# Layout of an intermediate array: G kept rows first and fields last in a CIN tower

## The chip, the cores and the metric

The kernel runs on one core of one Trainium2 chip. A core has five engines that run side by side: TensorE (PE in the profile, with its weight loads as PEld), VectorE (DVE), ScalarE (ACT), GpSimd (POOL) and SyncE (SP), which here issues DMAs. TensorE's clock is granted at one of two levels, 1.2 or 2.4 GHz; the profile gives it as a share of full speed. The metric is the device time of one execution, in microseconds.

## The reference, cut to what matters

2048 rows of ids select 39 embedding vectors of 16 floats each. Two compressed interaction layers and a small MLP follow:

```
e  = stack of 39 table rows                       # [2048, 39, 16]
x1 = einsum('bid,hi->bhd', e x e, W0)             # [2048, 128, 16]
x2 = einsum('bid,hi->bhd', x1 x e, W1)            # i runs over 128 * 39
z  = concat(x1.sum(-1), x2.sum(-1))               # [2048, 256]
h  = relu(concat(z, dense_ctx) @ W_top1 + b1)     # 512
h  = relu(h @ W_top2 + b2)                        # 256
y  = h @ W_top3
```

Since only the sum of x2 over the 16 dimensions is wanted, layer 1 can be had from `G[i, b, f] = sum_d x1[b, i, d] * e[b, f, d]`, as 39 matmuls of 128 x 128 weights, one for each field f. A fortieth "field" of ones (f = 39) gives the sum of x1 itself.

## The kernel before, in words

The 2048 rows are taken in 8 iterations of 256 rows (`NB`), each of 8 chunks (c = 0 to 7) of 32 rows, so 64 chunks in all. A chunk has 512 columns (32 rows x 16 dimensions) and 7 steps (k = 0 to 6).

For each step TensorE or a DMA places shifted copies of the embeddings, VectorE multiplies them (`multiply`, L739), ScalarE rounds the product (`round_product`, L572), VectorE forms the remainder (`lower_part`, L748), and TensorE contracts both against W0 in three matmuls of 512 columns (`contract`, L397, L398, L400). The result x1 is copied out (`copy_x1`, L577), transposed (`transpose_x1`, L412), and split (L581, L759) in the chunk after. In that chunk's steps 3 to 6, `make_g` (L429) multiplies it with a block diagonal of the embeddings, in four parts q of 8 rows each: three matmuls give 320 columns, 8 rows of 40 fields, in PSUM. `copy_g` (L589) on ScalarE copies each part into G. G is in SBUF with 128 partitions (i) and holds two iterations' rows, 512, of 40 fields; the halves are used in turn. There are 64 x 4 = 256 such copies.

One iteration later `layer1` (L440) reads G: one fp32 matmul for each of the 39 fields, with the 256 rows of an iteration as moving operand. The table `LAYER1` places them in the chunks: 7 fields in c = 1, 4 in c = 2, 8 in each of c = 3, 4 and 5, and 4 in c = 6. `mlp1` (L459) reads field 39 of G as moving operand for each of the four blocks of 128 of the first MLP layer, in c = 6 and 7; `mlp2` (L471) and `mlp3` (L480) run in c = 0 of the iteration after. Iteration 0 has no layer 1. The last iteration's layer 1 and MLP stand after all chunks, with nothing beside them.

A fp32 matmul of this program is two instructions on TensorE: 39 fields in 8 iterations are 312 calls, and the profile has 624 instructions of L440. The four G matmuls of `mlp1` are 64 instructions in the same way.

At c = 2 to 3 and c = 6 to 7 the embeddings of the next tile of 128 rows are split on VectorE (`split_hi`, L716, and `split_lo`, L722), transposed on TensorE (L368) and copied by ScalarE in four copies (`copy_eT`, L556). This happens for 15 tiles beside the chunks.

Each engine has its own instruction list, written out by hand in the order of these steps, and engines wait for each other's semaphores. The start of the kernel uses the memory of G as `staging` for weights, before any G is written.

Of the kernel before, what the change touches and what calls it, by code (L numbers as in the profile page):

```python
# [5 lines left out]
F = 39  # L22
D = 16
B = 2048
H = 128
# [6 lines left out]
CB = 32  # L32
# [4 lines left out]
NB = TB * TPI  # L37
ITERS = B // NB
Q = COLS // 128
QB = CB // Q  # L40
FO = F + 1
# [26 lines left out]
def after(engine, semaphore, value):  # L68

    if isinstance(value, int) and value <= 0:  # L70
        return
    engine.wait_ge(semaphore, value)
# [45 lines left out]
def cin_tower(nc, dense_t, ids, tables, w_top1, b_top1, w_top2, b_top2, w_top3, w0, w1,  # L118
# [5 lines left out]
    with ctx:  # L124
        def sb(name, shape, dt=f32):
            return ctx.enter_context(nc.sbuf_tensor(name, shape, dt))

        def ps(name, shape, dt=f32):
            return ctx.enter_context(nc.psum_tensor(name, shape, dt))

        def sem(name):
            return ctx.enter_context(nc.semaphore(name))
# [7 lines left out]
        w1T = sb("w1T", [H, F, H])  # L140
        wt1_cin = sb("wt1_cin", [128, 2, H1])

        wt1_dense = sb("wt1_dense", [3 * GAP, H1], f32r)
# [18 lines left out]
        x1T_lo = sb("x1T_lo", [128, Q, H], f32r)  # L162
        e_diag = [sb(f"e_diag{n}", [128, QB, Q, 2, FO], f32r) for n in range(2)]

        G = sb("G", [H, FO, 2 * NB])

        staging = G[:, :, :].rearrange("p f b -> p (f b)")
        w0_both = staging[0:ROWS, 0:2 * KT * H].rearrange("p (a k h) -> p a k h", a=2, k=KT)
        w0_sum = w0_both[:, 0, :, :]
        wt1_dense_f = staging[0:3 * GAP, 2 * KT * H + SELECTED:2 * KT * H + SELECTED + H1]  # L170
# [1 line left out]
        dense_parts = sb("dense_parts", [3 * GAP, NB], f32r)  # L172
# [13 lines left out]
        g_ps = [ps(f"g_ps{n}", [128, QB * FO]) for n in range(2)]  # L186
        mlp_ps = ps("mlp_ps", [128, 2, NB])
# [38 lines left out]
        g_ready = sem("g_ready")  # L226
# [129 lines left out]
        def _(pe):  # L356
# [76 lines left out]
            def layer1(it, fields):  # L433

                for j in fields:
                    if j == 0:

                        pe.wait_ge(g_ready, Q * CPI * (it + 1))
                        after(pe, y_ready, it)
                    last = nc.tensor.matmul(mlp_ps[:, 0, :], w1T[:, j, :], G[:, j, bass.ds(it % 2 * NB, NB)],  # L440
                                            start=(j == 0), stop=(j == F - 1))
                    if j == F - 1:
                        last.then_inc(z2_in_ps, 1)

            def mlp1(it, third):

                if third == 0:

                    pe.wait_ge(z2_ready, it + 1)
                    pe.wait_ge(dense_split, it + 1)  # L450
                if third == 3:

                    pe.wait_ge(h1_ready, it * M1 + 2)
                operands = ((wt1_cin[:, 0, :], G[:, F, bass.ds(it % 2 * NB, NB)]), (wt1_dense[:, :], dense_parts[:, :]),
                            (wt1_cin[:, 1, :], z2[:, :]))
                for n in (2 * third, 2 * third + 1):
                    m, part = n // 3, n % 3
                    weights, x = operands[part]
                    last = nc.tensor.matmul(mlp_ps[:, m % 2, :], weights[:, m * 128:(m + 1) * 128], x,  # L459
                                            start=(part == 0), stop=(part == 2))  # L460
                if third % 3 == 2:
                    last.then_inc(h1_in_ps, 1)
# [20 lines left out]
            def chunk(it, c, first=False, second=False, final=False):  # L483
# [6 lines left out]
                for k in range(KT):  # L490

                    for item in ITEMS_AT[k]:
                        if item < REPS:
                            replicate(it, c, item)
                        elif has_next:
                            replicate(*chunk_after(it, c), item - REPS)
                    if makes_eT and (c % CPT, k) in ET_STEPS:
                        if (c % CPT, k) == ET_STEPS[0]:

                            after(pe, x1T_lo_ready, it * CPI + c)  # L500
                        transpose_e(next_tile, ET_STEPS.index((c % CPT, k)))
                    if has_last:
                        if k == 1:
                            transpose_x1(*last, final and c >= CPT)
                        if k >= KT - Q:
                            make_g(*last, k - (KT - Q), final and c >= CPT)
                    if not first:
                        layer1(it - 1, fields_at(c, k))
                        if (c, k) in MLP1_STEPS:
                            mlp1(it - 1, MLP1_STEPS.index((c, k)))  # L510
                    if not first and not second:
                        if (c, k) in MLP2_STEPS:
                            mlp2(it - 2, MLP2_STEPS.index((c, k)))
                        if (c, k) == MLP3_STEP:
                            mlp3(it - 2)
                    contract(it, c, k)
# [26 lines left out]
            for q in range(Q):  # L543
                make_g(end, CPI - 1, q)
            layer1(end, range(F))
            for n in range(len(MLP1_STEPS)):
                mlp1(end, n)
# [5 lines left out]
        def _(act):  # L553
# [29 lines left out]
            def copy_g(it, c, q):  # L583

                if q == Q - 1:
                    act.wait_ge(e_diag_free, it * CPI + c + 3)
                else:
                    act.wait_ge(g_in_ps, (it * CPI + c) * (Q - 1) + q + 1)
                nc.scalar.copy(G[:, :, bass.ds(it % 2 * NB + c * CB + q * QB, QB)].rearrange("i f b -> i b f"),  # L589
                               g_ps[q % 2][:, :].rearrange("i (b f) -> i b f", f=FO)).then_inc(g_ready, 1)  # L590

            def copy_z2(it):

# [23 lines left out]
            def chunk(it, c, first=False, second=False, final=False):  # L617
# [5 lines left out]
                for k in range(KT):  # L623
                    if k + 1 < KT:
                        round_product(it, c, k + 1)
                    elif has_next:
                        round_product(*chunk_after(it, c), 0)
                    if k == 0 and has_last:
                        copy_x1(*last)
                    if REPS in ITEMS_AT[k] and has_next:  # L630
                        copy_cycle(*chunk_after(it, c))

                    c1, k1 = (c, k - 1) if k else (c - 1, KT - 1)
                    if makes_eT and (c % CPT, k) in ET_STEPS:
                        copy_eT((c // CPT + 1) % TPI, next_tile, ET_STEPS.index((c % CPT, k)))
                    if k > KT - Q and has_last:
                        copy_g(*last, k1 - (KT - Q))
                    if k == 0 and not (first and c <= 1):
                        copy_g(*chunk_before(*last), Q - 1)
                    if not first and c1 >= 0:  # L640
                        if len(fields_at(c1, k1)) and fields_at(c1, k1)[-1] == F - 1:
                            copy_z2(it - 1)
                        if (c1, k1) in MLP1_STEPS[2::3]:
                            relu1(it - 1, MLP1_STEPS[2::3].index((c1, k1)))
                    if not first and not second and (c1, k1) == MLP2_STEPS[-1]:
                        relu2(it - 2)
                    if k == 1 and has_last:
                        round_x1T(*last)
                    if (c, k) == DENSE_STEP and not first:
                        round_dense(it - 1)  # L650
                    if (c, k) == MLP3_STEP and not first and not second:
                        copy_y(it - 2)
# [14 lines left out]
            for c in range(CPI):  # L667
                chunk(end, c, final=True)
            copy_x1(end, CPI - 1)
            copy_g(end, CPI - 2, Q - 1)  # L670
            relu2(end - 1)
            round_x1T(end, CPI - 1)
# [169 lines left out]
```

## Time and profile before

| | us |
|---|---|
| median of 3 runs | 965.97 |
| lowest, highest | 965.49, 969.34 |
| profiled execution: span of core 0 | 1508.4 |
| PE busy in it | 884.9 |
| DVE busy | 648.8 |
| ACT busy | 600.9 |
| mean granted TensorE clock | 0.788 |

For the profiled execution no time but its span is given. It is 542 us above the median of the timed runs: it has long stretches in which all engines stand still and for which the trace shows no releaser ("another core or an unknown queue" in the chain, "remote" or "issue" as releaser). The stretches between them run without a stop, and these are the ones to read. Durations of instructions overlap where an engine is pipelined, so the time that one really takes on its engine is read from start to start, or from the chain of waits, which counts each moment once.

### The profile page before, as it was taken

To read this page: it belongs to the slowest core of one execution; us is meant where nothing else is said; L and a number is where in the kernel's file an instruction comes from. 1 tells how busy PE (TensorE), PEld (TensorE's weight loads), DVE (VectorE), ACT (ScalarE), POOL (GpSimd) and SP (SyncE) were. 2 spreads that over 40 slices of the span, in tenths; PEclk is the share of its full clock that TensorE was granted. 3 is DMA by queue.
4 is the path that set the end of the run, shared out by engine and by line. 5 is a ranking of instruction groups with operands and counts; after the bars stand their busy time and mean duration, and the time that the engine had idled before them with its cause. 6 is when DMAs were issued, how large, how long until landed. Compare 5 with 4: busy or idle time off the path is not lost.

```text
span 1508.4 us, 15925 instructions
## 1 busy us (share of the span) xinstructions
PE 884.9 (59%) x3824; PEld 686.1 (45%) x3824; DVE 648.8 (43%) x1012; ACT 600.9 (40%) x1033; POOL 623.7 (41%) x628
## 2 busy tenths in 40 slices
PE   0136393719268292763958367291863936629998
PEld 0014262508146181552846256270642724527886
DVE  2015292617155282442835156160632615427870
ACT  0013282407154171532735154160532714418772
POOL 6756437461714517154271715417054071450000
PEclk9997596759678596785977678595775967859999
DMA  4112142212122132122322122121221312203320
GB/s 130 24 39 61 38 113 52 69 45 66 26 75 61 23 98 68 38 52 51 85 59 58 27 77 71 39 67 25 78 59 18 95 27 70 67 13 101 106 78 3
DMA packets 101439, 88.81 MB, mean 59 GB/s; under 512 B 59925, under 2 KB 71325, under 8 KB 101250
## 3 DMA queue, kind: packets, MB, share of 16 engines
q1 hardware_dynamic: 81410, 83.02, 18.8%
q0 software_dynamic: 19968, 5.15, 3.9%
q14 instruction: 45, 0.37, 0.1%
q8 instruction: 16, 0.26, 0.1%
HBM read 21.35 MB, written 10.49 MB: 21 GB/s over the span
## 4 chain that ended last, share of the span: by engine, by line
PE 38%; another core or an unknown queue 28%; issue 20%; ACT 6%; DVE 4%; POOL 2%; DMA 1%; DVEq 0%; ACTq 0%; SPq 0%; POOLq 0%
PE mlp_ps L440 7%; PE g_ps L429 6%; PE x_ps L400 5%; PE x_ps L397 5%; PE x_ps L398 5%; PE rep_ps L386 3%; POOL e_rows L346 2%; ACT G L589 2%; PE mlp_ps L471 2%; PE mlp_ps L459 2%; DVE products L739 2%; ACT product_hi L572 2%; DVE product_lo L748 1%; PE aux_ps L368 1%
## 5 line engine op out<-in xcount | busy, mean ns | idle before, releaser
L346 POOL DMA_INDIRECT e_rows<-in_tbl_dram,ids_sb x624 | 623.5, 999 | 721.3 <-DMA ids_sb<-in_ids_dram 535.7
L748 DVE TENSOR_TENSOR product_lo<-products,product_hi 117x512 fp32r<-117x512 f32 (+1 forms) x448 | 308.1, 688 | 598.7 <-remote 369.6
L572 ACT CAST product_hi<-products 117x512 fp32r<-117x512 f32 (+1 forms) x448 | 281.4, 628 | 298.7 <-remote 131.2
L400 PE MATMUL x_ps<-product_lo,w_hi 117*128 117x512 f32 (+1 forms) x448 | 199.3, 445 | 176.0 <-issue 91.8
L397 PE MATMUL x_ps<-product_hi,w_hi 117*128 117x512 f32 (+1 forms) x448 | 254.7, 569 | 9.9 <-issue 9.9
L589 ACT COPY G<-g_ps 128x320 f32 (+1 forms) x256 | 189.4, 741 | 38.2 <-remote 24.6
L400 PEld LDWEIGHTS x_ps<-product_lo,w_hi 117*128 117x128 f32 (+1 forms) x448 | 92.5, 207 | 224.1 <-issue 104.5
L398 PE MATMUL x_ps<-product_hi,w_lo 117*128 117x512 f32 (+1 forms) x448 | 190.3, 425 | 0.0
L429 PE MATMUL g_ps<-e_diag,x1T_hi 128*128 128x320 f32 x512 | 134.7, 347 | 92.6 <-issue 58.9
L440 PE MATMUL mlp_ps<-G,w1T 128*128 (+1 forms) x624 | 186.8, 400 | 0.8 <-ACT G L589 0.8
L429 PEld LDWEIGHTS g_ps<-e_diag,x1T_hi 128*128 128x128 f32 x512 | 97.6, 206 | 126.9 <-issue 82.7
L368 PE MATMUL aux_ps<-ident,e_parts 128*80 128x128 f32 x256 | 47.3, 316 | 178.1 <-ACT eT L556 84.5
L556 ACT CAST eT<-aux_ps 80x512 fp32r<-80x512 f32 x64 | 67.5, 1054 | 198.8 <-issue 95.0
L739 DVE TENSOR_TENSOR products<-rep_ps,left 117x512 f32<-117x512 f32 x192 | 131.1, 683 | 33.2 <-issue 20.4
L386 PE MATMUL rep_ps<-eT,select_r 80*117 80x512 f32 (+1 forms) x256 | 117.9, 461 | 41.4 <-issue 22.9
L739 DVE TENSOR_TENSOR products<-shifted,left 117x512 f32<-117x512 f32 (+1 forms) x192 | 131.7, 686 | 0.2
L368 PEld LDWEIGHTS aux_ps<-ident,e_parts 128*80 128x80 f32 x256 | 31.6, 137 | 198.2 <-issue 151.6
L440 PEld LDWEIGHTS mlp_ps<-G,w1T 128*128 128x128 f32 x624 | 115.7, 201 | 11.4 <-ACT G L589 1.0
L412 PE MATMUL aux_ps<-ident,x 128*128 128x128 f32 x256 | 45.7, 308 | 113.0 <-issue 104.0
L397 PEld LDWEIGHTS x_ps<-product_hi,w_hi 117*128 117x128 f32 (+1 forms) x448 | 93.8, 209 | 25.1 <-issue 13.5
L398 PEld LDWEIGHTS x_ps<-product_hi,w_lo 117*128 117x128 f32 (+1 forms) x448 | 94.5, 211 | 11.5
L759 DVE TENSOR_TENSOR x1T_lo<-aux_ps,x1T_hi 128x512 fp32r<-128x512 f32 x64 | 44.3, 692 | 118.5 <-issue 60.5
(42 smaller groups left out, 612.7 us busy)
## 6 DMA issues: line engine op xcount, KB each, us to landing
shifted<-cycle SPq DMA_DIRECT2D x128, 234.0 KB
left<-cycle SPq DMA_DIRECT2D x192, 78.0 KB
e_scratch<-e_parts SPq DMA_DIRECT2D x16, 640.0 KB
e_diag<-e_scratch SPq DMA_DIRECT2D x512, 20.0 KB
e_rows<-in_tbl_dram,ids_sb POOLq DMA_INDIRECT x624
shifted<-cycle SPq DMA_DIRECT2D x64, 156.0 KB
w1T<-in_L_rec_W_dram SPq DMA_DIRECT2D x1, 2496.0 KB
G<-in_L_rec_W_dram SPq DMA_DIRECT2D x1, 819.0 KB
```

The source lines that it names most:

```text
L346: nc.gpsimd.indirect_dma_start(out=e_rows[slot][:, f * D:(f + 1) * D], out_offset=None, in_=tables[f], in_offset=bass.IndirectOffsetOnAxis ...
L368: last = nc.tensor.transpose(aux_ps[0:2 * FO, m * TB:(m + 1) * TB], e_parts[:, n * DPB + m, :, :].rearrange("b q f -> b (q f)"), ident[:, :])
L386: nc.tensor.matmul(rep_ps[rep_bank(c, item)][0:rows, :], select_r[:, item:item + rows], columns(c), start=True, stop=True).then_inc(rep_in ...
L397: nc.tensor.matmul(x1_ps[c % 2][:, :], w0_hi[0:rows, k, :], product_hi[0:rows, slot, :], start=(k == 0), stop=False)
L398: nc.tensor.matmul(x1_ps[c % 2][:, :], w0_lo[0:rows, k, :], product_hi[0:rows, slot, :], start=False, stop=False)
L400: last = nc.tensor.matmul(x1_ps[c % 2][:, :], w0_hi[0:rows, k, :], product_lo[0:rows, (c * KT + k) % LO_RING, :], start=False, stop=(k == ...
L429: last = nc.tensor.matmul(g_ps[q % 2][:, :], x[:, q, :], e_diag[c % 2][:, :, q, part, :], start=(n == 0), stop=(n == 2))
L440: last = nc.tensor.matmul(mlp_ps[:, 0, :], w1T[:, j, :], G[:, j, bass.ds(it % 2 * NB, NB)], start=(j == 0), stop=(j == F - 1))
L572: nc.scalar.copy(product_hi[0:rows, n % RING, :], products[0:rows, n % RING, :]).then_inc(hi_ready, 1)
L589: nc.scalar.copy(G[:, :, bass.ds(it % 2 * NB + c * CB + q * QB, QB)].rearrange("i f b -> i b f"), g_ps[q % 2][:, :].rearrange("i (b f) -> ...
L739: nc.vector.tensor_tensor(products[0:rows, n % RING, :], x[0:rows, :], left[c % 2][0:rows, :], ALU.mult).then_inc(product_ready, 1)
L748: nc.vector.tensor_tensor(product_lo[0:rows, n % LO_RING, :], products[0:rows, n % RING, :], product_hi[0:rows, n % RING, :].bitcast(f32), ...
```

## The change

G is declared with the rows ahead of the fields. ScalarE's copy then writes 320 consecutive floats where it wrote each float 2048 bytes from the one before it (within a row's 40 fields). TensorE's moving operand for a field, which was 256 consecutive floats, is now 256 floats with 160 bytes from one to the next. The size of G, the staging area, the order of all instructions and all semaphores are as they were.

```diff
-        G = sb("G", [H, FO, 2 * NB])
-
-        staging = G[:, :, :].rearrange("p f b -> p (f b)")
+        G = sb("G", [H, 2 * NB, FO])
+
+        staging = G[:, :, :].rearrange("p b f -> p (b f)")
...
-                    last = nc.tensor.matmul(mlp_ps[:, 0, :], w1T[:, j, :], G[:, j, bass.ds(it % 2 * NB, NB)],
+                    last = nc.tensor.matmul(mlp_ps[:, 0, :], w1T[:, j, :], G[:, bass.ds(it % 2 * NB, NB), j],
                                             start=(j == 0), stop=(j == F - 1))
...
-                operands = ((wt1_cin[:, 0, :], G[:, F, bass.ds(it % 2 * NB, NB)]), (wt1_dense[:, :], dense_parts[:, :]),
+                operands = ((wt1_cin[:, 0, :], G[:, bass.ds(it % 2 * NB, NB), F]), (wt1_dense[:, :], dense_parts[:, :]),
                             (wt1_cin[:, 1, :], z2[:, :]))
...
-                nc.scalar.copy(G[:, :, bass.ds(it % 2 * NB + c * CB + q * QB, QB)].rearrange("i f b -> i b f"),
-                               g_ps[q % 2][:, :].rearrange("i (b f) -> i b f", f=FO)).then_inc(g_ready, 1)
+                nc.scalar.copy(G[:, bass.ds(it % 2 * NB + c * CB + q * QB, QB), :].rearrange("i b f -> i (b f)"),
+                               g_ps[q % 2][:, :]).then_inc(g_ready, 1)
```

## Rows read from the trace of the kernel before

**Rows 1.** The page: span, busy time of each engine, shares of the chain.

```profile
span 1508.4 us, 15925 instructions
...
PE 884.9 (59%) x3824; PEld 686.1 (45%) x3824; DVE 648.8 (43%) x1012; ACT 600.9 (40%) x1033; POOL 623.7 (41%) x628
...
PE 38%; another core or an unknown queue 28%; issue 20%; ACT 6%; DVE 4%; POOL 2%; DMA 1%; DVEq 0%; ACTq 0%; SPq 0%; POOLq 0%
```

**Rows 2.** Stretches: start:end, length, engines' busy time and instructions, PE clock, DMA.

```profile
194.53:203.99 9.46, 9.28 (x43) 6.41 (x42) 9.19 (x17) 7.94 (x16) 0.00 (x0) 1.00 0.40 112
1186.23:1200.55 14.32, 14.31 (x61) 11.16 (x61) 10.10 (x17) 9.21 (x18) 0.00 (x0) 0.88 0.27 74
1388.27:1399.28 11.01, 11.01 (x56) 9.51 (x55) 9.46 (x15) 8.09 (x14) 0.00 (x0) 1.00 0.27 73
1399.28:1412.13 12.85, 12.66 (x68) 9.77 (x67) 11.18 (x17) 10.28 (x17) 0.00 (x0) 1.00 0.39 112
1412.13:1423.69 11.56, 11.39 (x57) 9.59 (x56) 9.46 (x15) 8.94 (x16) 0.00 (x0) 1.00 0.40 117
1435.15:1446.60 11.45, 11.45 (x58) 9.89 (x57) 9.47 (x15) 8.19 (x14) 0.00 (x0) 1.00 0.29 79
1457.74:1467.73 9.99, 9.99 (x52) 8.46 (x51) 6.97 (x11) 7.68 (x16) 0.00 (x0) 1.00 0.20 53
1476.85:1493.97 17.12, 17.10 (x78) 14.73 (x78) 0.41 (x1) 0.41 (x1) 0.00 (x0) 1.00 0.01 2
```

**Rows 3.** Chain of waits, 1435 to 1447: start, us on the chain, what.

```profile
1435.34 0.87 PE mlp_ps L440 x4
1436.21 0.23 PE x_ps L397
...
1437.13 0.44 PE aux_ps L412 x4
...
1440.06 0.43 PE g_ps L429 x3
```

**Rows 4.** Chain of waits, 1406 to 1414.

```profile
1407.16 0.77 ACT G L589
1407.94 0.24 ACT product_hi L572
...
1408.26 1.07 ACT eT L556
1409.33 0.56 ACT G L589
1409.88 0.26 ACT product_hi L572
...
1411.27 0.57 ACT G L589
```

**Rows 5.** Groups by line and shape: count, busy us, mean ns, idle before.

```profile
L589 ACT COPY G<-g_ps 128x320 f32 x160 | 118.6, 741 | 31.2 <-remote 22.4 <-issue 5.6 <-PE g_ps L429 2.8
...
L577 ACT COPY x<-x_ps 128x512 f32<-128x512 f32 x64 | 37.4, 585 | 136.1 <-remote 82.8 <-issue 29.7 <-PE x_ps L400 23.5
...
L722 DVE TENSOR_TENSOR e_parts<-e_rows,e_parts 128x624 f32<-128x624 f32 x16 | 19.6, 1222 | 0.0
...
L716 DVE CAST e_parts<-e_rows 128x624 fp32r<-128x624 f32 x16 | 11.4, 716 | 39.9 <-DMA e_rows<-in_tbl_dram,ids_sb 39.9
...
L596 ACT COPY h<-mlp_ps 128x256 f32<-128x256 f32 x8 | 3.3, 411 | 15.8 <-PE mlp_ps L440 15.8
...
L698 DVE TENSOR_TENSOR G<-G 117x896 f32<-117x896 f32 x1 | 1.1, 1093 | 0.0
...
L706 DVE TENSOR_TENSOR wt_dense<-G,wt_dense 32x512 fp32r<-32x512 f32 x1 | 0.7, 684 | 0.0
...
L700 DVE CAST w_hi<-G 117x896 fp32r<-117x896 f32 x1 | 0.6, 627 | 0.0
...
L704 DVE CAST wt_dense<-G 96x512 fp32r<-96x512 f32 x1 | 0.4, 416 | 0.0
```

## The prediction, made before the changed kernel was run

> **What bounds the kernel now.** I read the page first. The span is 1508.4 us against a median of 966, and the chain names an unknown releaser or "issue" for 48% of it [rows 1]. Busy shares of the span therefore say little: 884.9 us of PE is 59% of this span but 92% of 966. So I looked for stretches without a stop and cut them at the starts of the copy of x1, which comes once per chunk; one stretch is then one chunk [rows 2].
>
> The last iteration shows seven such chunks at full granted clock (1.00). The chunk at 1388.27 is c = 1 (11.01 us), 1399.28 is c = 2 (12.85), 1412.13 is c = 3 (11.56), 1435.15 is c = 5 (11.45) and 1457.74 is c = 7 (9.99). PE is busy for the whole of c = 1 and c = 5, while ACT has 8.1 to 8.2 us and DVE 9.5 us. Busy PE can still be a PE that waits, so the chain of waits decides: in c = 5 it stays on PE from matmul to matmul. A 512-column matmul of the contraction holds it for 0.23 us, three 320-column ones 0.43 to 0.45, and four layer-1 instructions 0.87, so 0.217 each [rows 3]. The sum of a chunk with 8 fields: 21 contractions and 4 replications at 0.23 are 5.75 us, 12 for G 1.8, 4 transposes 0.44 [rows 3], 16 for layer 1 3.47. That is 11.46, and the stretch is 11.45. TensorE bounds these chunks, and what is added to a matmul there is added to the time.
>
> Chunk c = 2 is another case. Its sum for PE, with 8 instructions of layer 1 and 12 transposes of e, is about 11.0, yet it takes 12.85, and from 1407 to 1412 the chain runs on ACT: copy of G, rounding of a product, copy of eT, again and again, with 0.56 us of each round on the copy of G [rows 4]. An eT group is made for 15 tiles. Iteration 0 has no layer 1, and there DVE is busy 9.19 of 9.46 us [rows 2]: neither side of the change reaches it but through that same ACT queue.
>
> These stretches account for most of the timed 966 us. Seven iterations of 92 to 99 us (the last one's chunks, and in the loop more at its turn, as in the 14.32 us of a c = 0) and iteration 0 at 9.46 us a chunk [rows 2], with some 118 us ahead of the first copy of x1 and 41 behind the last come to about 916; I take the other 50 as lying around the span or as small stops. The differences below apply to the profiled span and the median alike (1508.4 and 966), as the unexplained stops hold none of the instructions that change.
>
> **Part 1, ScalarE's copy.** 256 copies of 128 x 320 now take 741 ns each. Copies from PSUM that write in one piece take 411 ns for 256 columns and 585 for 512 [rows 5]: 0.68 ns a column, which gives an estimate of 455 for 320. So a copy shortens by 286 ns, and ACT loses 73 us of busy time. In chunks on PE's chain this is worth nothing: the copies lie beside matmuls, and the next part of G waits for the copy two parts before, 1.5 us earlier. On the ACT chain of an eT group three copies stand: at most 3 x 0.286 = 0.86 us, at least 0, since DVE (11.18 busy) and PE (11.0) are next. Both lie 1.7 us below the 12.85, so I take most of it, 0.7. Over 15 groups that is 10.5 us gained, with ends 0 and 12.9.
>
> **Part 2, TensorE's reads.** 688 instructions (624 of layer 1, 64 of mlp1) read 256 fp32 values, consecutive before and 160 bytes apart after. A column of these takes 0.217 us / 256 = 0.85 ns; a contraction's takes 0.23 / 512 = 0.45 [rows 3]. No row shows TensorE reading apart, so I bound it by the other engines. VectorE's subtraction L722 reads one operand 64 bytes apart: 624 elements in 1222 ns. The consecutive ones take 1093 ns for 896 and 684 for 512, so 1.065 ns an element and 139 fixed; for L722 that leaves 1.74 ns an element. The cast L716 reads the same way with one operand: consecutive casts, 627 ns for 896 and 416 for 512, have 0.55 ns an element and 135 fixed, so 581 / 624 = 0.93 ns. The scattered copy of G writes an element every (741 - 237) / 320 = 1.58 ns, with the fixed part of the other copies [rows 5]. So:
> - Low end: TensorE gets a value in less than its 0.85 ns a column already, and the reads cost nothing.
> - Cast's rate: 0.93 ns, +0.02 us an instruction.
> - Subtraction's rate: 1.74 ns, and an instruction takes 0.445 instead of 0.217: +0.23. The scattered copy's 1.58 ns gives +0.19.
> - High end: its 0.85 ns a column may hide two fetches of each value (a contraction's column needs half the time). At 1.74 ns each that is 0.89 us an instruction, +0.67.
>
> The nearest is the pair in the middle, two rows of fp32 data in which each element is far from the next. The same price comes from two fetches at 0.85 to 0.93 ns. I take 1.70 ns and +0.216 us, double the present time.
>
> The Trainium skill, Advanced Engine Details and Errata, section Memory Cachelines, says that SBUF is read in lines of 16 bytes, that two hits on a line are needed to hide the access, and that a new line at every access costs a penalty; it gives no size. Here every value would be in a line of its own, where four shared one. The rows on VectorE and ScalarE agree in direction, and they disagree among themselves on size (0.93 against 1.74). By that rule the copies gain and the matmuls lose; without it only the copies' gain would be left. FP8 and Floating Point Precision, section TensorE Precision Notes, says that true fp32 is four passes through the array. With two instructions a call, as the counts here show, that would be two passes in each. Whether a pass fetches its values again, neither page nor trace tells.
>
> **Sum.** Per iteration with layer 1: c = 1 has 14 instructions, c = 3, 4 and 5 have 48; all 62 on PE's chain: 13.4 us. c = 2 and 6 have 16 and mlp1 8 more in c = 6 and 7: 24 x 0.216 = 5.2, of which I let half vanish in the slack of the ACT stretches: 2.6. Together 16.0, for 7 iterations 112. Behind the last chunk, 78 instructions stand bare, 17.12 us now [rows 2], and 8 of mlp1: 86 x 0.216 = 18.6. Less the 10.5 of part 1: +120. So 966 + 120 = 1086 for the median, and 1508 + 120 = 1628 for a profiled span with the same stops. What is late next in the chunks is nothing new: PE holds the chain for longer, ACT and DVE wait more. No wait is added and no queue changes.
>
> **Rivals.**
> - A, the reads are free, and the kernel is faster: a value comes within 0.85 ns. For it: the cast's 0.93 ns is nearly there, and fp32 columns have double the time of the contraction's. Against it: L722. Then only part 1 is left: 966 - 10.5 = 955.5, in a range of 950 to 963.
> - B is my forecast, 1086; by itself 1055 to 1115 (1.58 to 1.74 ns; none or all of the 5.2 us hidden).
> - C, two slow fetches: 688 x 0.65 = 447, less 10 and a little hidden: about 1395. It needs the high end twice, which no row asks for.
> - D, a small price between free and double. At the cast's rate, 0.02 x 688 = 13 us, less 10.5: 968. At half of B's price, 0.108: about 1020.
> - E, the copy doesn't shorten because what slows it is the read of PSUM and not the write. The read is consecutive in both kernels, so I give it no more than a few in 100, inside the others; it takes the 10.5 away.
>
> Slower than before is decided by one thing: above some 0.02 us more an instruction (0.93 ns a column) the matmuls eat the copies' gain.
>
> **How the numbers follow.** B 0.42, A 0.37, D 0.13, C 0.08. Within 0.5%, 4.8 us, is about what a measurement of this kernel can't tell from no change. A is faster by more than that in 0.30 and not in 0.07; D is half way to the same in 0.04; the rest is slower: 0.30, 0.11, 0.59. The likeliest is B: 1086 us. The range has to reach A: 953 to 1110, which leaves out C, A's lowest edge and B's highest. B alone would be 1055 to 1115.
>
> **What would show it.** In the profile after: L589 near 455 ns (not 741), which decides E. Four instructions of L440 on the chain 1.74 us instead of 0.87, the 78 bare ones in 34 us instead of 17.12, and a chunk with 8 fields 14.9 us instead of 11.45: B. Unchanged 0.87 and 17.12 would be A, 2.6 or more C. Iteration 0 stays at 9.5 us. In an eT chunk, ACT off the chain and less than 12.85 us would confirm part 1 in A; in B the chain there moves to PE. The prediction is wrong if L440's spacing stays below 0.3 us.

## The result and the profile after

The changed kernel took 1104.03 us (median of 4 runs, 1100.08 to 1105.47) against 965.73 for the kernel before (4 runs, 963.87 to 969.34): a ratio of 1.1428, with an interval of 1.1394 to 1.1462. That is 138 us slower. Forecast were 1086 us, and 953 to 1110 as the range.

Lines of the code stand 16 lower in the profile after: L424 is what was L440, L573 was L589, L330 was L346. The page of the changed kernel first (busy time and share by engine, the clock in 40 slices, the head of the chain by engine):

```profile
span 1103.7 us, 15925 instructions
...
PE 981.1 (89%) x3824; PEld 657.0 (60%) x3824; DVE 656.1 (59%) x1012; ACT 539.8 (49%) x1033; POOL 647.1 (59%) x628
...
PEclk9997979999989999999999999999999999999999
...
PE 76%; POOL 15%; issue 7%; ACT 1%; DVE 0%; DMA 0%; DVEq 0%; ACTq 0%; POOLq 0%
```

This execution has no long stops, unlike the first one of the kernel before [rows 1], so its span can be set beside the timed runs. PE has 76% of the chain.

The two edits show in the groups by line of the changed kernel (count, busy us, mean ns):

```profile
L573 ACT COPY G<-g_ps 128x320 f32 x160 | 69.9, 437 | 2.9
...
L443 PE MATMUL mlp_ps<-G,wt_cin 128*128 x40 | 23.6, 681 | 0.2
```

The copy takes 437 ns, where [rows 5] had 741 and the estimate was 455. For the matmuls the mean is not the occupancy, so the chain of waits is the view, here in a chunk c = 5 of the changed kernel (start, us on the chain):

```profile
998.01 2.00 PE mlp_ps L424 x4
1000.00 0.23 PE x_ps L381
...
1000.94 0.44 PE aux_ps L396 x4
1001.38 0.99 PE mlp_ps L424 x2
```

Four instructions of layer 1 hold TensorE for 2.00 us; in [rows 3] four held it for 0.87. Everything else between them is unchanged: 0.23 a contraction, 0.44 for four transposes. The stretches of the changed kernel that answer to [rows 2] (length, busy time by engine, clock, DMA) are one whole iteration, c = 5 in it, the c = 2 of the last iteration, and the bare 78 instructions of the end:

```profile
680.26:803.52 123.26, 120.52 (x479) 81.86 (x479) 81.34 (x127) 67.35 (x130) 80.48 (x78) 0.99 0.33 85
755.71:771.71 16.00, 16.00 (x58) 10.25 (x57) 9.74 (x15) 7.22 (x15) 12.19 (x12) 1.00 0.28 71
951.45:965.90 14.45, 14.25 (x67) 9.86 (x66) 11.31 (x17) 9.69 (x17) 0.00 (x0) 1.00 0.34 105
1047.78:1087.04 39.26, 39.24 (x78) 16.44 (x78) 0.41 (x1) 0.41 (x1) 0.00 (x0) 1.00 0.01 2
```

The 78 instructions take 39.26 us instead of 17.12, so 0.503 each instead of 0.219: a price of 0.284 us. With 16 of them a chunk of 8 fields should grow by 4.54 us, and it grew from 11.45 to 16.00, by 4.55. The c = 2 of the last iteration grew from 12.85 to 14.45. The clock is at its upper level (1.00) in the two chunks and at the end, and PE is busy for 14.25 of the 14.45 us, so the chain has moved to it there.

But 688 instructions at 0.284 us are 195 us, and the kernel lost 138. The copies' gain is small; some 50 us are missing. That became the main question.

### The profile page after: what moved, and what is told of

Same layout as the page of the kernel before. It is cut to its first block, busy times and chain, and to the rows that moved or that the text cites. A ratio compares the mean times of both kernels' runs of the same rounds, so it can differ in the third digit from the quotient of the medians.

```text
span 1103.7 us, 15925 instructions
## 1 busy us (share of the span) xinstructions
PE 981.1 (89%) x3824; PEld 657.0 (60%) x3824; DVE 656.1 (59%) x1012; ACT 539.8 (49%) x1033; POOL 647.1 (59%) x628
## 4 chain that ended last, share of the span: by engine, by line
PE 76%; POOL 15%; issue 7%; ACT 1%; DVE 0%; DMA 0%; DVEq 0%; ACTq 0%; POOLq 0%
PE mlp_ps L424 27%; POOL e_rows L330 15%; PE g_ps L413 8%; PE x_ps L381 8%; PE x_ps L384 8%; PE x_ps L382 8%; PE rep_ps L370 5%; PE mlp_ps L443 4%; PE mlp_ps L455 3%; PE aux_ps L352 2%; PE aux_ps L396 2%; PE mlp_ps L464 1%; ACT h L590 0%; DVE products L723 0%; ACT G L573 0%
## 5 line engine op out<-in xcount | busy, mean ns | idle before, releaser
L330 POOL DMA_INDIRECT e_rows<-in_tbl_dram,ids_sb x624 | 646.9, 1037 | 283.7 <-issue 186.8
L556 ACT CAST product_hi<-products 117x512 fp32r<-117x512 f32 (+1 forms) x448 | 279.5, 624 | 314.8 <-PE x_ps L384 176.0
L424 PE MATMUL mlp_ps<-G,w1T 128*128 (+1 forms) x624 | 351.4, 674 | 0.5 <-ACT G L573 0.5
L381 PE MATMUL x_ps<-product_hi,w_hi 117*128 117x512 f32 (+1 forms) x448 | 311.7, 696 | 0.0
L384 PE MATMUL x_ps<-product_lo,w_hi 117*128 117x512 f32 (+1 forms) x448 | 180.5, 403 | 1.6 <-DVE product_lo L732 1.2
L382 PE MATMUL x_ps<-product_hi,w_lo 117*128 117x512 f32 (+1 forms) x448 | 179.3, 400 | 0.0
L370 PE MATMUL rep_ps<-eT,select_r 80*117 80x512 f32 (+1 forms) x256 | 108.7, 425 | 53.5 <-DVE products L723 49.9
L424 PEld LDWEIGHTS mlp_ps<-G,w1T 128*128 128x128 f32 x624 | 112.8, 195 | 45.4 <-issue 37.9
L413 PE MATMUL g_ps<-e_diag,x1T_hi 128*128 128x320 f32 x512 | 122.7, 321 | 0.3 <-issue 0.2
L573 ACT COPY G<-g_ps 128x320 f32 (+1 forms) x256 | 111.4, 435 | 4.2 <-PE g_ps L413 1.2
L370 PEld LDWEIGHTS rep_ps<-eT,select_r 80*117 80x117 f32 (+1 forms) x256 | 47.8, 187 | 78.8 <-DVE products L723 61.0
L413 PE MATMUL g_ps<-e_diag,x1T_lo 128*128 128x320 f32 x256 | 80.0, 312 | 0.0
```

Of the source, the lines that this page charges most:

```text
L330: nc.gpsimd.indirect_dma_start(out=e_rows[slot][:, f * D:(f + 1) * D], out_offset=None, in_=tables[f], in_offset=bass.IndirectOffsetOnAxis ...
L370: nc.tensor.matmul(rep_ps[rep_bank(c, item)][0:rows, :], select_r[:, item:item + rows], columns(c), start=True, stop=True).then_inc(rep_in ...
L381: nc.tensor.matmul(x1_ps[c % 2][:, :], w0_hi[0:rows, k, :], product_hi[0:rows, slot, :], start=(k == 0), stop=False)
L382: nc.tensor.matmul(x1_ps[c % 2][:, :], w0_lo[0:rows, k, :], product_hi[0:rows, slot, :], start=False, stop=False)
L384: last = nc.tensor.matmul(x1_ps[c % 2][:, :], w0_hi[0:rows, k, :], product_lo[0:rows, (c * KT + k) % LO_RING, :], start=False, stop=(k == ...
L413: last = nc.tensor.matmul(g_ps[q % 2][:, :], x[:, q, :], e_diag[c % 2][:, :, q, part, :], start=(n == 0), stop=(n == 2))
```

## The experiments

Two theories were set against each other. **P** is the account of the prediction: TensorE, and ScalarE in the eT groups, bound the kernel before. **G** was formed from the profile after: the gather on GpSimd bounds the kernel before in its timed runs, and part of what the matmuls now take was waiting for gathered rows before.

**The two halves of the change, alone.** For the copy alone, the reads were made consecutive again:

```diff
-                    last = nc.tensor.matmul(mlp_ps[:, 0, :], w1T[:, j, :], G[:, bass.ds(it % 2 * NB, NB), j],
+                    last = nc.tensor.matmul(mlp_ps[:, 0, :], w1T[:, j, :], G_flat[:, bass.ds(it % 2 * (NB * FO) + j * NB, NB)],
...
```

(The operand of `mlp1` is changed in the same way.)

> The copy of G writes in one piece as after the change; TensorE reads 256 consecutive values as before it, from the same half of G, so the values it takes belong to other fields and rows and the output is not the reference's. Theory P (the prediction's account: TensorE and, in the eT groups, ScalarE bound the kernel before): copies of 435 ns instead of 741, 10.5 us less, about 955.5 us. Theory G (in the timed runs the gather on GpSimd bounds the kernel before: 39 gathers of about 1.34 us a tile are 52 us, 104 us an iteration of two tiles, and an unstopped iteration of the rest takes only 92 to 99): the copies lie in that slack, and the time stays within 3 us of 966.

Measured: 964.63 us (958.26 to 968.69, 10 runs) against 969.71, ratio 0.9952 (0.9917 to 0.9987). For the reads alone, the copy scatters again:

```diff
-                nc.scalar.copy(G[:, bass.ds(it % 2 * NB + c * CB + q * QB, QB), :].rearrange("i b f -> i (b f)"),
-                               g_ps[q % 2][:, :]).then_inc(g_ready, 1)
+                rows = G_halves[:, bass.ds(it % 2, 1), :, c * CB + q * QB:c * CB + (q + 1) * QB]
+                nc.scalar.copy(rows.rearrange("i h f b -> i h b f"),
+                               g_ps[q % 2][:, :].rearrange("i (h b f) -> i h b f", h=1, f=FO)).then_inc(g_ready, 1)
```

> TensorE reads values 160 bytes apart as after the change; the copy of G scatters as before it (1024 bytes apart, within one iteration's half of G), so the output is not the reference's. Theory P: the reads alone cost what the whole change costs plus the 10.5 us that the copies give: about 1114 us. Theory G: TensorE bounds every chunk once its reads are slow, ScalarE's queue is hidden, and the time is within 5 us of the changed kernel's 1104. Both: L424's instructions 0.50 us apart on the chain.

Measured: 1109.41 us (1108.62 to 1113.91, 4 runs), ratio 1.1457 (1.1382 to 1.1533). The whole loss is in the reads. Both halves fall between the theories: a gain of 5 us from the copy (the interval is 1 to 8) where P said 10.5 and G up to 3, and 1109 where P said 1114 and G 1104 within 5. The intervals leave out P's 10.5 for the copy, but a gain smaller than forecast doesn't name what bounds the kernel, so these two runs don't settle the base.

**Another profile of the kernel before.** No edit.

> The kernel before, unchanged, for a profile without the long stops of the first. Theory P: span about 950, chunks with 8 fields of 11.45 us throughout, the iteration at 92 to 99 us, GpSimd idle between tiles. Theory G: the same chunks, but an iteration of 104 us, GpSimd without a pause from its first gather to its last near 840 us, and VectorE's split waiting for gathered rows once or twice an iteration.

Measured: 962.99 us, span 961.2. This execution has none of the stops. Its line of the gather, and whom VectorE waited for, from its groups by shape:

```profile
L346 POOL DMA_INDIRECT e_rows<-in_tbl_dram,ids_sb x624 | 658.2, 1055 | 192.8 <-issue 188.7 <-DMA ids_sb<-in_ids_dram 4.1
...
L716 DVE CAST e_parts<-e_rows 128x624 fp32r<-128x624 f32 x16 | 11.2, 699 | 109.3 <-DMA e_rows<-in_tbl_dram,ids_sb 109.1
```

GpSimd idles 188.7 us in gaps of 0.3 between gathers and only 4.1 us for ids: 658.2 + 192.8 = 851 us without a pause, 53 a tile and 106 an iteration. VectorE's split of e waits 109.1 us for gathered rows, of which 39.9 are the first tile, at the start of the kernel. Two chunks of this execution, a c = 5 and the c = 6 after it, which holds a split:

```profile
674.59:686.04 11.45, 11.45 (x58) 9.90 (x57) 9.54 (x15) 8.27 (x15) 9.01 (x9) 1.00 0.39 92
686.04:707.01 20.97, 15.79 (x69) 12.49 (x68) 11.26 (x17) 10.75 (x18) 16.09 (x17) 0.84 0.41 111
```

The first is the chunk of [rows 2]; the second takes 20.97 us, where the same kind of chunk takes 13.28 in the next experiment. PE is busy for 15.79 us of it, where such a chunk of the next experiment has PE busy for 13.29, and the granted clock of this stretch is 0.84: for a part of it the clock is at its lower level, and the matmuls take longer. That is in the price of the wait too. The chain of waits between 300 and 850 us says the same (shares by line):

```profile
by line: POOL e_rows L346 44.0%; issue 17.3%; PE g_ps L429 4.3%; PE mlp_ps L440 4.0%; PE x_ps L400 3.8%; PE x_ps L397 3.8%; PE x_ps L398 3.7%; PE rep_ps L386 2.9%; PE mlp_ps L471 2.1%; PE mlp_ps L459 2.0%; DMA ids_sb<-in_ids_dram 1.4%; DMA 
```

**Fewer gathers, in both kernels.** From the second iteration on, 20 of 39 gathers a tile, with the semaphore values to match:

```diff
-                    for f in range(F):
+                    for f in range(fields):
...
-                sp.wait_ge(gathered[slot], (it + 1) * (16 * F))
+                sp.wait_ge(gathered[slot], it * (16 * GATHERED) + 16 * F)
```

> The kernel before with 20 of 39 gathers per tile from the second iteration on (the other fields keep old rows, so the output is not the reference's); semaphore values to match. GpSimd's 104 us an iteration fall to about 54. Theory G: the time falls from 966 to the sum of unstopped stretches, 900 to 920 us. Theory P: the gathers are hidden anyway, and the time stays within 5 us of 966.

> The changed kernel with 20 of 39 gathers per tile from the second iteration on, in the same way (output not the reference's). Both theories: TensorE bounds it, so the time stays within 10 us of 1104. Under Theory G the difference to the run before it is then the whole price of the reads less the copies' gain, 688 x 0.283 = 195 us less about 10: 185 us, where the full kernels differ by only 138. Under Theory P it is the 138 of the full kernels.

Measured: the kernel before falls to 896.4 us (894.26 to 898.63, 4 runs; ratio 0.9283, 0.9240 to 0.9326) and the changed one to 1082.75 (1081.34 to 1085.2, 4 runs; ratio to the kernel before with all gathers 1.1215, 1.1165 to 1.1264). P allowed the first 5 us of change, and it was 69. G forecast 900 to 920 there, so the fall was 4 us larger than its range, and no change in the second; the second fell by 21, more than the 10 allowed. The reason is at the start: iteration 0 has no layer 1, so its chunks are short in both kernels, and the gather bounds the changed kernel there too. From copy of x1 to copy of x1, its iterations 0 and 1 took 112.1 and 131.5 us with all gathers and 99.6 and 122.0 with 20, the later ones 123 and 123. The difference of the two is 186 us against 138 with all gathers. An iteration of the kernel before with 20 gathers, and one of the changed kernel with 20, in their stretches, each with its c = 0 behind it:

```profile
564.86:663.59 98.73, 96.39 (x478) 78.63 (x478) 79.81 (x127) 74.39 (x131) 42.26 (x40) 1.00 0.38 103
564.86:577.55 12.69, 12.68 (x61) 9.95 (x61) 9.96 (x17) 9.21 (x18) 0.00 (x0) 1.00 0.29 78
```

```profile
658.32:781.03 122.71, 120.33 (x479) 81.83 (x479) 81.13 (x127) 67.34 (x130) 41.66 (x40) 0.99 0.30 83
658.32:672.35 14.03, 14.03 (x61) 11.08 (x61) 10.09 (x17) 8.28 (x18) 0.00 (x0) 0.88 0.26 74
```

98.7 us is less than the 106 of two full tiles' gathers; 122.7 is more. The c = 0 chunks read nothing from G, and yet one takes 1.34 us more: its granted clock was 0.88. So 1.3 of the 24 us between these two iterations are clock and not reads. A c = 0 of 14 us is no mark of the reads: with 20 gathers it comes in four of the five iterations 1 to 5 of the changed kernel and in two of those of the kernel before. And the chain of the kernel before with 20 gathers, 300 to 780 us, has no gather in it:

```profile
by line: PE mlp_ps L441 16.1%; PE g_ps L430 12.9%; PE x_ps L401 11.8%; PE x_ps L398 11.6%; PE x_ps L399 11.4%; PE rep_ps L387 7.6%; issue 6.9%; PE mlp_ps L460 3.8%; PE mlp_ps L472 3.6%; PE aux_ps L413 3.2%; ACT G L590 2.7%; PE aux_ps L369 2
```

So theory G stands and P falls as to the base. The unloaded difference, 186, is the reads' 195 less some 6 to 9 for the copies. Even the 896 us hold some of the gather's wait: tile 1 is still gathered whole, and VectorE waits 13.6 us for it in the c = 2 of iteration 0.

**The copy without the gather in front.** The copy in one piece and consecutive reads, with 20 gathers.

> Copy in one piece, consecutive reads (values of other fields and rows), and 20 of 39 gathers from the second iteration on: part 1 of the change without the gather's cover. To be set against the kernel before with 20 gathers, 896 us. The prediction's term of 10.5 us (0.7 us in each of 15 eT groups) holds if it is 884 to 888; if ScalarE's queue is worth less than the chain of waits suggested, 890 to 896.

Measured: 890.37 us (890.06 to 891.69, 4 runs). The ratio to the full kernel before, timed beside it, is 0.9197 (0.9166 to 0.9228) here and 0.9283 (0.9240 to 0.9326) for scattered copies. That is 6.0 us less in medians, just inside the range of the weaker account, and 8.3 by the ratios. The c = 2 chunks shrink by half a microsecond, not by 0.7, and those of c = 6 by 0.3; over 7 iterations that is 5.8. A c = 2 with scattered copies, and one with copies in one piece:

```profile
489.82:502.71 12.89, 12.85 (x68) 9.85 (x67) 11.23 (x17) 10.30 (x18) 9.85 (x10) 1.00 0.44 117
```

```profile
486.97:499.34 12.37, 12.30 (x67) 9.66 (x66) 11.35 (x17) 9.55 (x17) 9.49 (x10) 1.00 0.40 109
```

This run and the changed kernel with 20 gathers differ only in TensorE's reads: 890.37 against 1082.75, or 192 us in medians and 195 in the ratios. That is the full 688 times 0.284, with nothing hidden.

**What the distance costs.** Layer 1's fields read with eight different steps, and fp32r matmuls are added at the end.

```diff
+                    if j < 5:
+                        last = nc.tensor.matmul(mlp_ps[:, 0, :], x, apart(it, 1), **ends)
+                    elif j < 10:
+                        last = nc.tensor.matmul(mlp_ps[:, 0, :], x, apart(it, 2), **ends)
...
+            for n in range(12):
+                nc.tensor.matmul(x1_ps[n % 2][:, 0:NB], w0_hi[0:ROWS, n % KT, :], narrow(10), start=True, stop=True)
```

> Layout as after the change, but the 39 layer-1 matmuls read G with other steps between values: fields 0 to 4 with 4 bytes, then five fields each with 8, 16, 20, 32, 40, 80 and the last four with 160 bytes (wrong values, so the output is not the reference's). At the very end 72 extra matmuls of 256 fp32r columns read an fp32r tile with steps of 4, 8, 16, 20, 32 and 40 bytes. Theory Lines (a value in a new 16-byte line costs a fixed time): 0.22 us an instruction at 4 and 8 bytes, 0.50 from 16 bytes on, alike for 16 to 160. Theory Distance (cost grows with the step): 16 to 40 bytes stay below 0.35 us and 160 is the dearest. On the fetches: if an fp32 instruction fetches each value twice, the fp32r matmul (half the time per column when consecutive, about 0.11 to 0.12 us) takes 0.25 us with values apart; if it fetches each once, the fp32r one takes 0.50 us like the fp32 one.

The one run took 1069.59 us. The chain of waits over the bare part at the end has, in order, steps of 4, 8, 16, 20, 32, 40, 80 and 160 bytes for fp32 (L434 to L448), then 4, 8, 16, 20, 32 and 40 for fp32r (L559 to L569):

```profile
1004.23 2.43 PE mlp_ps L434 x10
1006.66 2.25 PE mlp_ps L436 x10
1008.91 4.53 PE mlp_ps L438 x10
1013.44 4.57 PE mlp_ps L440 x10
1018.00 4.61 PE mlp_ps L442 x10
1022.62 4.53 PE mlp_ps L444 x10
1027.15 5.33 PE mlp_ps L446 x10
1032.48 4.01 PE mlp_ps L448 x8
...
1051.84 1.60 PE x_ps L559 x12
1053.44 2.75 PE x_ps L561 x12
1056.19 2.80 PE x_ps L563 x12
...
1064.35 3.20 PE x_ps L569 x12
```

For fp32: 0.225 us an instruction at 8 bytes, close to the 0.219 of the consecutive reads in [rows 2] (the first ten here, 0.243 each, include the start of the stretch), then a jump to 0.453 at 16, flat to 40 (0.453 to 0.461), 0.533 at 80 and 0.501 at 160. Theory Lines holds for the place of the jump; its claim of one price for all steps does not, as 80 and 160 bytes cost 0.05 to 0.08 more. For fp32r the jump comes already at 8 bytes: 0.133 to 0.229.

**The same tile, both types.** To exclude that the two types differed by tile, fp32 and fp32r matmuls read one tile with steps of 4, 8, 12 and 16 bytes.

```diff
+                nc.tensor.matmul(x1_ps[n % 2][:, 0:NB], w1T[0:ROWS, n, :], narrow(2).bitcast(f32), start=True, stop=True)
...
+                nc.tensor.matmul(x1_ps[n % 2][:, 0:NB], w0_hi[0:ROWS, n % KT, :], narrow(2), start=True, stop=True)
```

> The kernel before, with matmuls of 256 columns added at the very end that all read the same tile (e_diag) with steps of 4, 8, 12 and 16 bytes: first as fp32 (12 instructions each), then as fp32r (12 each). Told apart: whether fp32 and fp32r differ by tile or by type. By type: fp32 0.22, 0.22, 0.22 to 0.45, 0.45 us; fp32r 0.12, 0.23, 0.23, 0.23. By tile: fp32 on this tile shows a cost at 8 bytes already. If an fp32 instruction fetched every value twice in two passes like the fp32r one, 8 bytes would cost it 2 x 0.23 = 0.46; if that stays 0.22, the account of two plain passes is out.

The one run took 996.27 us. The chain at its end, fp32 first (L556 to L562), then fp32r (L564 to L570):

```profile
969.38 2.79 PE x_ps L556 x12
972.16 2.70 PE x_ps L558 x12
974.87 4.08 PE x_ps L560 x12
978.95 5.44 PE x_ps L562 x12
984.38 1.40 PE x_ps L564 x12
985.79 2.74 PE x_ps L566 x12
988.53 2.81 PE x_ps L568 x12
991.34 2.80 PE x_ps L570 x12
```

It is by type. fp32: 0.233, 0.225, 0.340 and 0.453 us. At 8, 12 and 16 bytes 256 values lie in 128, 192 and 256 lines of 16 bytes, and the times are 1.76, 1.77 and 1.77 ns a line. Consecutive values lie in 64 lines and take nearly as long as at 8 bytes, so there something other than the lines sets the time. fp32r: 0.117, 0.228, 0.234 and 0.233, which is 0.9 ns a value for any step but 4 (the run before had 0.218 us at 32 bytes and 0.267 at 40), and no price by lines. The time of fp32 at 8 bytes stays at 0.225, so two plain passes that each pay what fp32r pays (0.46) are out. What makes the two types differ is left open.

**Pairs.** The rate at 8 bytes points to a layout between the two, fields in pairs:

```diff
-        G = sb("G", [H, 2 * NB, FO])
+        G = sb("G", [H, FO // 2, 2 * NB, 2])
...
-                    last = nc.tensor.matmul(mlp_ps[:, 0, :], w1T[:, j, :], G[:, bass.ds(it % 2 * NB, NB), j],
+                    last = nc.tensor.matmul(mlp_ps[:, 0, :], w1T[:, j, :], G[:, j // 2, bass.ds(it % 2 * NB, NB), j % 2],
...
-                nc.scalar.copy(G[:, bass.ds(it % 2 * NB + c * CB + q * QB, QB), :].rearrange("i b f -> i (b f)"),
-                               g_ps[q % 2][:, :]).then_inc(g_ready, 1)
+                nc.scalar.copy(G[:, :, bass.ds(it % 2 * NB + c * CB + q * QB, QB), :].rearrange("i g b s -> i b g s"),
+                               g_ps[q % 2][:, :].rearrange("i (b g s) -> i b g s", g=FO // 2, s=2)).then_inc(g_ready, 1)
```

> A layout between the two: G is [H, 20, 512, 2], fields in pairs, so that TensorE reads 256 values 8 bytes apart (0.22 us an instruction in the run on steps, as when consecutive) and ScalarE writes pairs, 160 separate places a copy where the kernel before has 320. The whole computation is done. If a place costs ScalarE what it does in the kernel before, half of 306 ns is saved: about 590 ns a copy. Theory G: the gather still bounds the kernel, the gain is part of the 5 us that the copy alone gave: 961 to 966 for 966, a ratio of 0.995 to 1.000. Theory P: about 5 us, 961. If 8 bytes cost TensorE in layer 1 after all, it is above 1000.

Measured: 970.42 us (966.09 to 978.8, 12 runs) against 968.88, ratio 1.0023 (0.9994 to 1.0052): no gain over the kernel before. Its groups by shape show the copy's new price and the wait for rows, and its chain shows the 78 bare instructions of layer 1:

```profile
L573 ACT COPY G<-g_ps 128x320 f32 x160 | 73.3, 458 | 0.9
...
L700 DVE CAST e_parts<-e_rows 128x624 fp32r<-128x624 f32 x16 | 11.2, 698 | 128.2 <-DMA e_rows<-in_tbl_dram,ids_sb 128.2
```

```profile
938.15 17.86 PE mlp_ps L424 x78
```

The copy takes 458 ns and not 590: writing two floats together takes almost all of the scatter's price away. TensorE pays a little: 17.86 us for the 78 instructions that took 17.12, so 0.229 each instead of 0.219, an estimate of 6.5 us for all 688. VectorE waits 128.2 us for gathered rows, 19 more than in the second profile of the kernel before. GpSimd's own unbroken time, busy and idle, and the span were 851.0 and 961.2 us in that profile, 856.0 and 965.7 with the copy alone, and 860.0 and 970.5 here: each time the span is 110 us more than the gather's, and the differences between the three are how fast the gathers went. The 5 us of the copy alone therefore can't be found in the profiles. So the same layout was run with 20 gathers, beside the kernel before with 20.

> The layout in pairs with 20 of 39 gathers from the second iteration on (the other fields keep old rows). If the pairs give what the copy in one piece gives where no gather stands in front: 889 to 892 us, as the run with copies in one piece (890) and 5 to 7 below the kernel before with 20 gathers (896). If the pairs gain nothing even there: 894 to 899.

> The kernel before with 20 of 39 gathers again, on the same chip as the run with pairs, so that the two can be compared: 894 to 899 us.

Measured: 894.73 us (893.63 to 895.79, 4 runs) and 897.94 (897.33 to 899.21, 4 runs). That is 3.2 us less, and the two sets of runs don't overlap; the ratios to the full kernel, 0.9221 (0.9173 to 0.9269) and 0.9255 (0.9207 to 0.9303), do. The time itself lies in the range that was expected if the pairs gain nothing (894 to 899), and the difference of 3.2 falls short of the 5 to 7 that were expected if they gain what the copy in one piece does. The slightly dearer reads would explain that: the copy in one piece with consecutive reads had 890.37. No version run here with all its gathers is surely faster than the kernel before by over 0.5%.

## Why the prediction came out as it did

**The likeliest case was the right one.** Case B, reads at about double the time of a matmul, was forecast at 1086 us, and 1104 came; the 2.00 us of four instructions are 2.3 times the 0.87 before. Cases A (free), C (two slow fetches, 1395) and D are out by the same 2.00 us. E is out by the copy's 437 ns.

**The price of an instruction was mis-sized**: 0.216 us forecast, 0.284 measured. VectorE's subtraction, at 1.74 ns a value [rows 5], was a good neighbour for steps of 16 to 40 bytes (0.453 / 256 = 1.77 ns). It says nothing of the further 0.05 us an instruction at 160 bytes; no row with such a distance between reads was there. The cast's 0.93 ns was the wrong neighbour for fp32; fp32r with steps of 12 and 16 bytes has that rate (0.91).

**The sum over an iteration was mis-sized as well.** Without the gather's cover an iteration grew from 98.7 to 122.7 us, by 24, where 16.0 was forecast. At the measured price, the 62 instructions on PE's chain are 17.6 us, and the 24 others 6.8; the copies give back 0.8 (c = 2 and c = 6), and the lower clock in c = 0 adds 1.3 in the pair compared, together 24.9 for the 24.0 measured. "I let half vanish" was too kind: of the 24 others' 6.8 us some 0.9 vanished at most, and the 192 to 195 us between the two runs that differ only in the reads leave as little. With faster copies PE is busy for 12.30 of the 12.37 us of a c = 2, so no slack is left there for slower reads. The bare end grew by 22.1 for its 78 instructions alone, where 18.6 was forecast for 86.

**The step that failed is the first one**, "These stretches account for most of the timed 966 us". The prediction summed them to 916 and took "the other 50 as lying around the span or as small stops". Around the span lie 1.8 us (962.99 timed, 961.2 of span), and there are no small stops. The 916 also hold 118 us ahead of the first copy of x1, where the undisturbed profile has 81.3, and 9.46 us for every chunk of iteration 0, where c = 2 takes 27.6 even with 20 gathers. With 20 gathers the kernel takes 896 us, and the other 70 were the gather, which ran without a pause. Its numbers stood in the groups by line of that first profile (count, busy us, mean ns, idle before and its releasers):

```profile
L346 POOL DMA_INDIRECT e_rows<-in_tbl_dram,ids_sb x624 | 623.5, 999 | 721.3 <-DMA ids_sb<-in_ids_dram 535.7 <-issue 185.6
```

623.5 us busy and 185.6 of issue gaps are 809 us for 16 tiles, 101 an iteration, more than the 92 to 99 of the chunks. The prediction cut out stretches between stops and summed them, and so cut out the engine whose work had been done during the stops. In that execution GpSimd waited 535.7 us for ids, which looked like slack; in the undisturbed one it waited 4.1.

**The two errors offset each other.** The forecast was 130.6 us for the reads (112 and 18.6), less 10.5 for the copies. Without the gather's cover the reads cost 195 and the copies give 6 to 9. The gather cost the kernel before 69 us and the changed one 21, so 48 us of its wait were taken up by slower matmuls: 195 - 9 - 48 = 138, the measured loss. (This is the four runs set side by side, not a test of its own.) The forecast of 120 was near in part by luck: the reads were put 64 us too low, and the gather's 48 us were put at nothing.

**ScalarE's part.** 10.5 us were forecast, 6.0 measured without the gather's cover, and 5 with it (0.9952, 0.9917 to 0.9987). The price per eT group was mis-sized: 0.7 us in each, where c = 2 gained 0.5 and c = 6 only 0.3. In the changed kernel a good part of the gain remains, though PE has the chain. Here is a c = 2 of the run with the reads alone, and one of the changed kernel:

```profile
708.33:723.20 14.87, 14.85 (x67) 10.02 (x66) 11.37 (x17) 10.37 (x18) 11.52 (x12) 1.00 0.37 100
```

```profile
709.53:723.88 14.35, 14.32 (x67) 9.94 (x66) 11.35 (x17) 9.62 (x18) 11.20 (x11) 1.00 0.39 101
```

It is 0.52 us shorter, and the c = 6 of the same iteration 0.19: 5 us over 7 iterations. In the timed runs, 1109 against 1104 is 5.4 us in medians and 2.8 in the ratios, whose intervals overlap, so there it isn't shown.

The rule on lines of 16 bytes (the Trainium skill, Advanced Engine Details and Errata, section Memory Cachelines) came true in direction and place: fp32 at 8 bytes, two values in a line, is nearly free (0.229 us against 0.219), and at 16 bytes, one value in a line, the time doubles (0.453). fp32r already pays at 8 bytes, with two values in each line, 0.228 us against 0.117; there the measurement differs from the rule of two hits a line, and the measurement decides.

What stays open: why 80 bytes cost more than 160, why fp32r pays by value and fp32 by line, and what stopped the first profiled execution of the kernel before.

## What to carry to other kernels

When a layout is chosen between a writer and a reader, keep consecutive what the engine on the chain reads, and test a middle way: pairs of floats gave ScalarE almost its full gain (458 against 437 ns) and cost TensorE 0.01 us an instruction, where the full change cost it 0.284. Before summing stretches of a profile with stops, add up each engine's own unbroken work over the whole program and divide by the iterations; GpSimd's 809 us would have shown the bound. A second profile, without stops, shows it at once. A slow-down of one engine costs less than its sum where another one held the bound (138 us instead of 186 here), and a speed-up under such a bound shows as little or nothing (5 us for the copy alone, none for the pairs).

## What the runs showed of the hardware

- TensorE, 256 moving fp32 values an instruction: 0.219 us consecutive, 0.225 to 0.229 at 8 bytes apart, 0.340 at 12, 0.453 to 0.461 at 16 to 40, 0.533 at 80, 0.501 at 160. All at a granted clock of 1.00. fp32r: 0.117 consecutive, 0.228 at 8 bytes, 0.233 at 16, 0.218 at 32, 0.267 at 40.
- ScalarE, 320 floats from PSUM to SBUF: 437 ns in one piece, 458 in pairs, 741 one by one. Scattering 1024 bytes apart took 740, as 2048 did.
- GpSimd, indirect gathers of 128 rows of 64 bytes: 0.94 us at the median and 1.06 in the mean, with 0.30 between two.
- TensorE's clock: a c = 0 chunk of the same 61 instructions took 12.69 us at a granted clock of 1.00 and 14.03 at 0.88. The chunks ahead of the two had PE busy for 12.21 of 14.26 us and 13.07 of 15.40; these rows don't show why only one was followed by the lower clock.
